# Head attention of a conv and attention block: values mixed by quarters of the queries, one key tile in each step, sums copied out by VectorE alone

## The reference, cut to what matters

```python
router_in = hidden_states.mean(axis=1)
logits = router_in @ Wr + br
_, top_idx = jax.lax.top_k(logits, K)                    # K = 6 of H = 12 heads
...
q = proj(Wq, bq) * m                                     # head dimension D = 32
k = proj(Wk, bk) * m
v = proj(Wv, bv) * m
scores = jnp.einsum('bhqd,bhkd->bhqk', q, k) / jnp.sqrt(jnp.float32(D))
probs = jax.nn.softmax(scores, axis=-1)
ctx = jnp.einsum('bhqk,bhkd->bhqd', probs, v)
ctx = ctx.transpose(0, 2, 1, 3).reshape(B, S, hid)
x = ctx @ Wo + bo + hidden_states                        # then a layer norm
```

## Time and profile before

| | |
|---|---|
| median of 3 runs | 3708.58 us (3705.68 to 3709.11) |
| the profiled execution | 3714.32 us, of which the span is 3712.5 us |
| mean granted clock of TensorE | 0.946 of full |
| PE busy | 3342.9 us (90%) |
| DVE busy | 2741.3 us (74%) |
| ACT busy | 2258.2 us (61%) |
| mixing, PE L2302 | 1536 instructions, 225.4 us busy |
| probabilities, ACT L2135 | 768 instructions, 417.1 us busy |
| maximum, DVE L1966 | 384 instructions, 469.4 us busy |

### The profile page before, as it was taken

The page is one execution under the profiler, slowest core; times in us unless marked ns, Lnnn a source line. Parts: engine busy times, 40 slices in busy tenths (PEclk is TensorE's granted clock), DMA queues, the critical chain, the costliest instruction groups (busy, mean ns, idle before and its releaser), DMA issues. The chain is left out here.

```text
span 3712.5 us, 65162 instructions
## 1 busy us (share of the span) xinstructions
PE 3342.9 (90%) x17998; PEld 1931.1 (52%) x17998; DVE 2741.3 (74%) x5161; ACT 2258.2 (61%) x5369; POOL 1399.3 (38%) x1487
## 2 busy tenths in 40 slices
PE   7969999999999999848999999968888888889887
PEld 4434444444444444437888888844444434434443
DVE  4468888888888888666888888846677677676766
ACT  4334444444444444355777777737877777777785
POOL 2144444444444444272222222210063453443535
PEclk9989999999999999968999999968999999999898
DMA  9999989899989999541000000021222322232221
GB/s 362 369 360 343 333 335 352 315 343 342 346 329 335 343 344 343 224 142 39 17 17 17 17 17 17 17 76 53 64 74 67 91 67 63 80 88 65 54 65 55
DMA packets 230567, 647.35 MB, mean 174 GB/s; under 512 B 31143, under 2 KB 127943, under 8 KB 229959
## 3 DMA queue, kind: packets, MB, share of 16 engines
q0 software_dynamic: 82944, 453.02, 32.5%
q1 hardware_dynamic: 147398, 191.91, 16.5%
HBM read 520.21 MB, written 79.18 MB: 161 GB/s over the span
## 5 line engine op out<-in xcount | busy, mean ns | idle before, releaser
L697 PE MATMUL b_acc<-b_sampled,b_w 128*128 128x512 f32 x2592 | 1211.4, 595 | 0.0
L632 DVE SCALAR_TENSOR_TENSOR b_mix<-shared,b_weight,b_mix 128x384 f32<-128x384 f32 x864 | 531.9, 621 | 140.4 <-ACT b_mix L655 82.9
L697 PEld LDWEIGHTS b_acc<-b_sampled,b_w 128*128 128x128 f32 x2592 | 449.4, 191 | 347.6 <-issue 347.6
L664 ACT ACTIVATE b_sampled<-b_tps 128x384 f32<-128x384 f32 x576 | 282.7, 491 | 566.1 <-PE b_tps L715 549.2
L1966 DVE TENSOR_REDUCE e_neg_top<-e_next 128x1 f32<-128x1024 f32 x384 | 469.4, 1223 | 210.8 <-PE e_next L2276 175.0
L632 DVE SCALAR_TENSOR_TENSOR b_mix<-b_got,b_weight,b_mix 128x384 f32<-128x384 f32 x864 | 530.9, 619 | 93.8 <-ACT b_mix L655 56.8
L2120 ACT ACTIVATE e_unused<-e_next,e_neg_top 128x1024 bf16<-128x1024 f32 x384 | 429.8, 1119 | 125.6 <-DVE e_neg_top L1966 113.2
L2135 ACT ACTIVATE e_prob<-e_s 128x512 f32<-128x512 f32 x768 | 417.1, 598 | 137.6 <-PE e_s L2288 135.2
L588 POOL DMA_INDIRECT shared<-corner_table,b_index x288 | 293.8, 1020 | 419.4 <-DVE b_mix L632 322.6
L588 POOL DMA_INDIRECT b_got<-corner_table,b_index x288 | 291.0, 1010 | 360.1 <-DVE b_mix L632 303.6
L715 PEld LDWEIGHTS b_tps<-ident,b_mix 128*128 128x128 f32 x1728 | 223.1, 142 | 372.6 <-issue 328.0
(11 more groups left out here) (221 smaller groups left out, 5315.3 us busy)
## 6 DMA issues: line engine op xcount, KB each, us to landing
corner_table<-y SPq DMA_DIRECT2D x32, 1536.0 KB, 14.8
e_stack<-e_high SPq DMA_DIRECT2D x384, 64.0 KB, 2.0
shared<-in_x SPq DMA_DIRECT2D x8, 1536.0 KB, 10.6
c_x<-in_x SPq DMA_DIRECT2D x16, 768.0 KB, 4.4
tokens<-y SPq DMA_DIRECT2D x64, 192.0 KB, 1.9
e_tok<-tokens SPq DMA_DIRECT2D x8, 1536.0 KB, 7.2
e_stack<-e_low SPq DMA_DIRECT2D x192, 64.0 KB, 2.0
shared<-tokens SPq DMA_DIRECT2D x8, 1536.0 KB, 7.3
```

Source lines behind the costliest of these rows:

```text
L632: ins = nc.vector.scalar_tensor_tensor(dst[:], src[:, q * C:(q + 1) * C], weight[g][:, q, k, i:i + 1], dst[:], ALU.mult, ALU.add)
L664: nc.scalar.activation(sampled[s % 2][:, :, i * P:(i + 1) * P], tps[t % 2][:, 0:C].rearrange("p (o q) -> p o q", q=P), ACT.Copy).then_inc( ...
L697: last = nc.tensor.matmul(acc[g][co][:], w_conv[:, k, ci, co * P:(co + 1) * P], sampled[s % 2][:, ci], start=(k == 0 and ci == 0), stop=(k ...
```

## The change

Now each call of the mixing handles one tile, and the four quarters of the array are the four quarters of the queries, 256 columns each, all with the same values as weights. Partitions 32i to 32i+31 of the bank then hold the whole sum of the 256 queries of quarter i; only 256 of its 512 columns are used. Tile c - 1 is mixed in step c, after the scores of c, at c3 to c7 and at c0 of the next head; c1 has no mixing, and c2 has two, tile 0 and tile 1. `odd`, its copy on ScalarE and its semaphore are gone; VectorE copies the four quarters to `ctx`, 32x256 each. ScalarE's wait before it writes over `prob` is taken for each tile (the tile four back must be mixed) and no longer for each pair.

```diff
-    PAIRS = STEPS // 2
+    QUARTERS = P // HD
+    QUARTER = PIX // QUARTERS
...
-                dve.sem_inc(pair_used, 2)
+                dve.sem_inc(tile_used, 4)
...
                 def heads_out(n, s, u):
                     g = head(n, s)
                     to = slice(HD * (s % 3), HD * (s % 3 + 1))
-                    dve.wait_ge(odd_out, g + 1)
-                    for f in range(2):
-                        last = nc.vector.tensor_tensor(ctx[u][to, s // 3, f * HALF:(f + 1) * HALF],
-                                                       odd[HD * (2 + f):HD * (3 + f)], b_acc[HD * f:HD * (f + 1)],
-                                                       ALU.add)
+                    dve.wait_ge(tile_used, STEPS * (g + 1) + 4)
+                    for i in range(QUARTERS):
+                        last = nc.vector.tensor_copy(ctx[u][to, s // 3, i * QUARTER:(i + 1) * QUARTER],
+                                                     b_acc[HD * i:HD * (i + 1), 0:QUARTER])
                     last.then_inc(acc_free, 1)
...
-                        if c % 2 == 0 and f == 0:
-                            act.wait_ge(pair_used, PAIRS * head(n, s) + c // 2 + 1)
+                        if f == 0:
+                            act.wait_ge(tile_used, STEPS * head(n, s) + c + 1)
...
-                def odd_copy(n, s):
-                    g = head(n, s)
-                    act.wait_ge(pair_used, PAIRS * (g + 1) + 2)
-                    act.wait_ge(acc_free, g + 1)
-                    nc.scalar.activation(odd[2 * HD:], b_acc[2 * HD:], ACT.Copy).then_inc(odd_out, 1)
...
-                            if c == 1 and (s or tail):
-                                odd_copy(*((n, s - 1) if s else (n - 1, KEPT - 1)))
...
-                def mix(n, s, u, pair):
+                def mix(n, s, u, c):
 
                     g = head(n, s)
-                    if pair == 0:
+                    if c == 0:
                         pe.wait_ge(acc_free, g + 1)
-                    pe.wait_ge(prob_ready, UNITS * g + 4 * pair + 6)
-                    for odd in range(2):
-                        c = 2 * pair + odd
-                        for f in range(2):
-                            at = HD * (2 * odd + f)
-                            last = nc.tensor.matmul(b_acc[at:at + HD], v[u][:, c, s], prob[(2 * c + f) % 8][:],
-                                                    start=(pair == 0), stop=(pair == PAIRS - 1))
-                    last.then_inc(pair_used, 1)
+                    pe.wait_ge(prob_ready, UNITS * g + 2 * c + 4)
+                    for i in range(QUARTERS):
+                        f, side = divmod(i, 2)
+                        last = nc.tensor.matmul(b_acc[HD * i:HD * (i + 1), 0:QUARTER], v[u][:, c, s],
+                                                prob[(2 * c + f) % 8][:, side * QUARTER:(side + 1) * QUARTER],
+                                                start=(c == 0), stop=(c == STEPS - 1))
+                    last.then_inc(tile_used, 1)
...
-                            if c == 0 and s:
-                                mix(n, s - 1, u, PAIRS - 1)
-                            elif c == 0 and tail:
-                                mix(n - 1, KEPT - 1, 1 - u, PAIRS - 1)
-                            elif c % 2 == 0 and c:
-                                mix(n, s, u, c // 2 - 1)
+                            if c == 2:
+                                mix(n, s, u, 0)
+                            if c >= 2:
+                                mix(n, s, u, c - 1)
+                            elif c == 1:
+                                pass
+                            elif s:
+                                mix(n, s - 1, u, STEPS - 1)
+                            elif tail:
+                                mix(n - 1, KEPT - 1, 1 - u, STEPS - 1)
```

More of the change, by code:

```diff
@@ L1489, in head_attention @@
         prob = [sb(mem, f"e_prob{i}", [HALF]) for i in range(8)]
-        odd = sb(mem, "e_odd", [HALF])
         ctx = [sb(mem, f"e_ctx{u}", [SIDES, PIX]) for u in range(2)]
@@ L1532, in head_attention @@
         prob_ready = sem("e_prob_ready")
-        pair_used = sem("e_pair_used")
+        tile_used = sem("e_tile_used")
         acc_free = sem("e_acc_free")
         t_tok_loaded = sem("e_t_tok_loaded")
-        odd_out = sem("e_odd_out")
         t_stats = sem("e_t_stats")
@@ L2172, in _ @@
                 turns(act, turn)
-                odd_copy(LAST, KEPT - 1)
                 def residual(k):
@@ L2364, in _ @@
                 turns(pe, turn)
-                mix(LAST, KEPT - 1, 1, PAIRS - 1)
+                mix(LAST, KEPT - 1, 1, STEPS - 1)
                 last = Fills(BATCH, FINAL)
```

## The result

| | before | after |
|---|---|---|
| median of 5 runs each | 3706.3 us (3703.2 to 3709.1) | 3726.8 us (3723.7 to 3730.3) |
| ratio | | 1.0046, interval 1.0035 to 1.0056 |
| the profiled execution | 3714.3 us | 3730.3 us |
| its mean granted clock of TensorE | 0.946 | 0.947 |

The changed kernel is slower by 0.46%, where 3715 was predicted. That is 12 us above the forecast and 3 above the forecast's own range (3706 to 3724), though within the range for 8 in 10 (3693 to 3740). The medians differ by 20.5 us, the ratio stands for 17; the loss is 17 to 20 us where I had forecast 6.

A forecast was written before the change was run, and what follows sets the result against it. It took a ring of TensorE, VectorE and ScalarE, none full, as the bound. Terms -30.7 + 10.3 + 12.8 + 9.3 - 0.7 = +1.0 us, +5 after cutting gains, gave 3715 us; 8-in-10 range 3693 to 3740.

The forecast's parts named there:

- Price of a mixing: Head attention, TensorE: a one-tile mixing takes 0.58 us instead of 1.01 for two tiles; two in a row 1.01.
- The line through the two rows: Profiled matmul groups of 512 and 128 columns (1.86 and 0.79 us) give 0.836 ns a column and 0.15 us fixed.
- the quarters don't run side by side: Rival: at 256 columns the four column quarters of a mixing run serially, 1.71 us each, +430 us; chance 0.02.
- Price of a copy: VectorE's 32x256 copy out of PSUM: 0.40 to 0.43 us each, four taken as 1.68 us a head.
- c3 and c5: Added mixings, +0.58 us each, mostly hide in fills' waits; uncovered where scores are on the chain, 22 times: +12.8 us.
- ScalarE's copy: Its removal frees 28 us of busy time, but VectorE's branch eats the gain; only -0.6 us at the stage's end.
- TensorE's terms: Mixings on the chain: c0, c4 and c6 together -30.7 us, c7 +10.3, c3 and c5 +12.8, c2 0.
- the cut of the gains by 5: Gains on the chain reduced by a sixth, +5 us, because a gain counts only until the next branch takes over.
- VectorE's copies: Four copies replace two additions, +0.31 us a head; c2's mixing waits for them 30 times: +9.3 us.
- The wait of the mixing: Sign of being right: c2's mixing waits for VectorE's copies some 20 to 30 us, up from 12.
- both lose: Rival: TensorE loses 0.30 us and VectorE 0.31 in each of 48 heads, +29 us, 3738; chance 0.30.
- second case: Case called likeliest by the rule that both ScalarE and VectorE should empty PSUM, since VectorE alone would do it afterwards.

The follow-up runs named there:

- experiment 7: Kernel before without ScalarE's copy of the odd tiles' sums; VectorE copies two 32x512 halves instead of adding, odd sums left out: 3713.1 us, ratio 1.0016.
- the pad behind: Kernel before plus one unused 32x160 VectorE addition per head, placed behind the two additions that free the accumulator: 3721.6 us, ratio 1.0038.
- experiments 3 and 4: Changed kernel with c2's mixings moved to c3 (3727.5 us, ratio 1.0050); changed kernel with VectorE's copies ahead of the maximum of c1 (3728.5, 1.0055).

## Why the prediction was near, and where it failed

- **Price of a mixing**: predicted 0.58, measured 0.57 to 0.64; two in a row predicted 1.01, measured 1.00 to 1.07 (the shorter numbers are pieces of the chain of waits, the longer ones whole groups in the timeline). The line through the two rows held at 256 columns, which it had no row for. That the quarters don't run side by side is refuted.
- **Price of a copy**: predicted 0.40 to 0.43, measured 0.419, four 1.68 as taken. That was right to the last digit kept.
- **c3 and c5**: the added mixings were to hide in the waits of row and output fills. These fell from 27.4 to 20.4 us in 18 cases and from 28.5 to 20.4 in 20, by 0.39 and 0.41 each: above the 0.3 that I had named as the sign, under the full 0.58. That agrees with an added mixing partly hidden; the profile doesn't exclude that the fills' waits fell for another reason.
- **ScalarE's copy**: predicted worth nothing inside the stage; experiment 7 measured 0.16% more time without it. The reason I gave (the maximum, not the copy, holds the additions) was read from one head; over the stage VectorE's additions waited for ScalarE's copy 11.0 us in only 3 cases, which bears it out. What ScalarE's freedom wins in experiment 7 it loses again: c0 is 20.5 us shorter, c1 to c3 are 19.4 longer.
- **TensorE's terms** (-30.7, +10.3 and +12.8, and the cut of the gains by 5): -2.6 us together. Undoing the spread gave -4 us with the copies on VectorE and +1 with them shared, so their sum is between +4 and -1, within noise of each other. The steps of the two profiles give most terms one by one: c4 -14.5 us (forecast -14.4), c6 -11.3 (-12.0), c7 +10.9 (+10.3), c3 and c5 together +8.8 (+12.8). Such close agreement is in part luck, since each is from one profile and the clock moved among the steps. The -4.3 of c0 can't be told apart, since c0 also holds what the removed ScalarE copy wins.
- **VectorE's copies: the step that failed.** I wrote that the mixing at c2 waits for them 30 times, and counted 30 x 0.31 = +9.3 us. With c0's -4.3 that made +5 us for c0 to c2; measured +19.4. With half of the copies off VectorE the time falls by 17 to 18 us (3726.8 against 3709.0). The size of one copy was right and the count wrong, because the way was wrong. I took the row of waits between copies and mixing as the list of heads in which VectorE's time counts. It counts wherever what stands behind the copies is late, and c0 to c2 grew in 40 of 48 heads. All 48 heads x 0.32 = 15.2 us of VectorE; the pad behind, 16.5 us of VectorE with the release unchanged, cost 11 to 14. The prediction did name what stands behind the copies on VectorE (a fill and the next maximum) and then priced only the release. That the time still fell into the wide range is no merit of this term: it was half of what it should have been, and the range was wide enough for the rival.
- **The wait of the mixing** was to grow from 12 us to some 20 to 30; it grew to 46 (from 13, counted in the same way). A wait can grow by more than it costs: experiments 3 and 4 took it to nothing or nearly (1.2 us) and gained nothing.
- **The rivals**: "both lose" had 3738, with +0.31 in all 48 heads on VectorE, which is close to what the runs show, and +0.30 on TensorE, which they don't. The time lies midway between that case and the forecast. The Trainium skill's rule ("TensorEngine Tiling (Array Packing)", section PSUM Bottleneck) to empty PSUM with both ScalarE and VectorE, which I had held to bear on the wait of c2 alone, bears on nearly every head: with the four copies split two and two between ScalarE and VectorE the loss vanished. (The prediction says that by this rule its "second case" would be likeliest; the case meant is the slower one, the first of its rivals.) The runs agree with it, with one bound: the split three and one did not do it, and all four on ScalarE could not be told from the kernel before.
- Two other differences between the profiles don't explain the loss. GpSimd's residual (`e_hb`) is waited for 23.7 us in 6 cases (13.2 before), but with shared copies it is 26.8 at the time of before. TensorE stood at 1.2 GHz for 162 us from the first exponential to the last after and for 161 before, in 21 stretches against 28. The prediction had named a count that changes by more than a few as a sign of being wrong; it did change, the sum of the time did not.

## What to carry to other kernels

Where several engines form a ring, price added work on an engine by everything that stands behind it in its queue, not by the one wait that names it: the row "mixing waits for copies" held 46 us, and emptying it changed nothing. A pad of the same length, put behind the release in the old kernel, prices the queue before anything is rewritten; but put it in more than one place, since here the same pad ahead of the release cost a third to a half as much, for a reason that is not known. Measure the length of each step in both profiles as well: it said in which steps and in how many heads the loss stood. And when work is taken off one engine only to be put on the other that shares in emptying an accumulator, ask which of the two the ring waits for: here 28 us less of ScalarE were worth nothing, and 15 us more of VectorE came with a loss of 17 to 20.

## What the runs showed of the hardware

- Matmuls in four column quarters, float32: 0.57 us for 8 instructions of 256 columns, 1.00 for 16. The second set costs 0.43, that is 0.84 ns a column, the first 0.14 us more.
- Out of PSUM, 32x256: VectorE's copy 0.414 to 0.419 us, ScalarE's 0.373 to 0.379. Cut into quarters, the accumulator costs VectorE 1.68 us by copies of 256 columns; two passes of 512 columns cost 1.36, by copy (0.680) or by addition (0.679) alike. Four times 0.419 against two times 0.680 is 0.16 us for each instruction more. A VectorE addition of 32x160 in SBUF took 0.343 us.
- Work removed need not gain time. Taking ScalarE's copy out (28 us of its busy time) gave +0.16% (0.04 to 0.27%).
- The granted clock of a run and its time move together: over the 74 runs of the kernel before, at 0.944 to 0.952, 0.001 less went with 1.5 us more. Which of them leads the other these runs don't show.
